# Autocorrelation attention and a merged feed-forward layer: rows added by an accumulating transfer, their low half on GpSimd, statistics' roots in batches, six late folds on TensorE

## The reference, cut

```python
def autocorrelation(Q, K, V):                     # heads H = 8, d = D // H
    corr = ifft(fft(q, axis=2) * conj(fft(k, axis=2))).real
    w, idx = top_k(corr.transpose(0, 1, 3, 2), int(2 * log(L)))
    w = softmax(w)
    for i in range(topk):
        out += w[..., i] * take_along_axis(v, minimum(idx[..., i] + pos, L - 1))

def ffn(x, W, bias, A, Bf, coeffs, scales):
    out = einsum('bsd,od->bso', x, W) + bias
    xa = einsum('bsd,erd->ebsr', x, A)
    return out + einsum('ebsr,eor,e->bso', xa, Bf, coeffs * scales)

x = x + autocorrelation(layernorm(x), ctx_4096, ctx_4096)
x = x + ffn(layernorm(x), L0_ffn_W, L0_ffn_bias, L0_ffn_A, L0_ffn_Bf, L0_ffn_coeffs, L0_ffn_scales)
```

## Time and profile before

| | |
|---|---|
| Median of three executions | 2596.8 us (2594.43 to 2602.17) |
| Profiled execution | 2623.54 us, its span 2621.7 us |
| TensorE busy | 2458.5 us, 94% of the span |
| VectorE, GpSimd, ScalarE busy | 1942.5, 2069.6, 1090.8 us |
| Prelude (windows 0 to 13) | 506.20 us |
| Steady part (windows 14 to 63) | 1823.30 us |
| Tail | 292.20 us |
| TensorE's mean granted clock | 0.98 |

### The profile page before, as it was taken

How to read it: one execution, slowest core, us unless ns; L and a number is a source line. 1 busy time by engine, 2 the same in 40 slices (tenths; PEclk the granted TensorE clock), 3 DMA queues, 4 the chain that set the end, 5 groups by cost and what they waited for, 6 DMA issues and landing times.

```text
span 2621.7 us, 36204 instructions
## 1 busy us (share of the span) xinstructions
PE 2458.5 (94%) x12288; PEld 1534.9 (59%) x12288; DVE 1942.5 (74%) x4526; ACT 1090.8 (42%) x2070; POOL 2069.6 (79%) x1430
## 2 busy tenths in 40 slices
PE   4999866899999979999999999997999999999999
PEld 3666555566666646666666666664666666654444
DVE  5888889778887798778887788779886788645000
ACT  4888856543444333543444344442433344211000
POOL 5799999778998779978997899788797889654222
PEclk8999978899999989999999999998999999999999
DMA  9399998967897677967897689966786687768853
GB/s 328 100 266 270 272 251 199 232 200 223 275 271 211 220 235 236 279 203 225 273 282 209 222 266 284 270 190 203 228 257 183 213 262 246 200 225 288 266 184 113
DMA packets 550025, 613.17 MB, mean 234 GB/s; under 512 B 322640, under 2 KB 448720, under 8 KB 532176
## 3 DMA queue, kind: packets, MB, share of 16 engines
q1 hardware_dynamic: 549840, 610.86, 77.8%
HBM read 383.22 MB, written 151.00 MB: 204 GB/s over the span
## 4 chain that ended last, share of the span: by engine, by line
PE 60%; POOL 16%; DMA 7%; DVE 6%; issue 5%; SPq 4%; ACT 2%; POOLq 0%; DVEq 0%; ACTq 0%
PE f_ps L834 12%; PE f_ps L836 12%; PE f_ps L838 12%; PE a_ps L706 8%; PE a_ps L751 4%; PE a_ps L799 3%; POOL f_x1p L1126 3%; PE a_ps L814 3%; PE a_ps L815 3%; POOL a_zu L1126 2%; POOL a_rows L1126 2%; POOL a_zvf L1126 2%; DMA a_w_lag<-a_w_row 2%; PE a_ps L756 1%; DVE a_twf L1251 1%
## 5 line engine op out<-in xcount | busy, mean ns | idle before, releaser
L834 PE MATMUL f_ps<-f_whi,f_hhi 128*128 128x512 f16 x2048 | 777.1, 379 | 5.8 <-issue 2.3
L836 PE MATMUL f_ps<-f_wlo,f_hhi 128*128 128x512 f16 x2048 | 776.9, 379 | 0.0
L838 PE MATMUL f_ps<-f_whi,f_hlo 128*128 128x512 f16 x2048 | 776.5, 379 | 0.0
L1126 POOL TENSOR_TENSOR a_zvf<-a_zvf,a_twf 128x512 f32<-128x512 f32 x256 | 340.6, 1361 | 115.8 <-DVE a_twf L1251 110.1
L918 ACT ACTIVATE a_side<-a_ps 128x1 f32<-128x1 f32 (+2 forms) x420 | 123.2, 331 | 543.6 <-PE a_ps L795 368.7
L838 PEld LDWEIGHTS f_ps<-f_whi,f_hlo 128*128 128x128 f16 x2048 | 200.6, 98 | 242.2 <-issue 1.1
L836 PEld LDWEIGHTS f_ps<-f_wlo,f_hhi 128*128 128x128 f16 x2048 | 200.6, 98 | 225.3 <-issue 0.8
L834 PEld LDWEIGHTS f_ps<-f_whi,f_hhi 128*128 128x128 f16 x2048 | 200.8, 98 | 219.7 <-issue 5.9
L1126 POOL TENSOR_TENSOR f_x1p<-f_x1p,f_y 128x512 f32<-128x512 f32 x128 | 170.9, 1368 | 100.1 <-DVE f_y L1251 100.1
L918 ACT ACTIVATE a_vu<-a_ps 128x512 f32<-128x512 f32 (+2 forms) x512 | 218.4, 489 | 73.4 <-PE a_ps L706 72.8
L751 PE MATMUL a_ps<-a_w_lag,lags 128*128 128x256 f16 x1536 | 234.8, 277 | 12.7 <-DMA a_w_lag<-a_w_row 11.5
(11 more groups left out here) (134 smaller groups left out, 5054.8 us busy)
## 6 DMA issues: line engine op xcount, KB each, us to landing
f_whi<-whi_scratch SPq DMA_DIRECT2D x128, 512.0 KB, 5.0
f_wlo<-wlo_scratch SPq DMA_DIRECT2D x128, 512.0 KB, 5.9
a_rows<-in_x_dram SPq DMA_DIRECT2D x62, 1024.0 KB, 8.6
vs<-in_ctx_dram SPq DMA_DIRECT2D x64, 512.0 KB, 6.2
xs<-in_x_dram SPq DMA_DIRECT2D x64, 512.0 KB, 7.6
parts_scratch<-a_so SPq DMA_DIRECT2D x64, 512.0 KB, 7.5
x_scratch<-a_rows SPq DMA_DIRECT2D x32, 1024.0 KB, 5.1
f_x1p<-x_scratch SPq DMA_DIRECT2D x32, 1024.0 KB, 6.6
```

Source lines behind the costliest of these rows:

```text
L834: nc.tensor.matmul(f_ps[:, t, :], h_hi[q][:, kq, rows_t], w_hi[u % WR][:, :, kq, :], start=(k == 0), stop=False)
L836: nc.tensor.matmul(f_ps[:, t, :], h_hi[q][:, kq, rows_t], w_lo[u % WR][:, :, kq, :], start=False, stop=False)
L838: mm = nc.tensor.matmul(f_ps[:, t, :], h_lo[q][:, kq, rows_t], w_hi[u % WR][:, :, kq, :], start=False, stop=(k == DB - 1))
L1126: return nc.gpsimd.tensor_tensor(whole, whole, part, op)
```

## The change

Four things change, and a fifth makes room.

1. `add_row` is no instruction of GpSimd any more. One transfer from GpSimd's own queue reads the attention's rows from `parts_scratch` and adds them to `a_rows` (`accum_op=ALU.add`). It is issued between `add_upper` and `add_lower`, and not behind `add_lower`. SP's two `load_attn` transfers per row tile, the tile `f_attn` and their waits go. `row_added` becomes two semaphores that the transfer counts up.
2. `row_low` goes from VectorE to GpSimd, right behind `add_products` and ahead of `add_group`. ScalarE's copy to PSUM goes.
3. `close_statistics` does four tiles at once, with 15 instructions on 128x4, at the end of `weights_low` in windows 5, 13, 21, 29, 37, 45 and 53. Its constants are tiles of SBUF now (`eps4`, `bits4`, `three_halves`), so that every one of these instructions reads two tiles of SBUF.
4. For the values of chunks 8 to 13, GpSimd leaves out the second level of sums and differences (2 instructions), and TensorE multiplies the first level with the matrix twice as often: 8 products and not 4 (`folded_once`, `fold_two`), with two negated matrices more in `fold`.
5. `p_bn`'s tiles lie in `a_side` now.

The core of the diff:

```diff
+UNFOLD_FROM = 8
...
+        def closed_batch(w):
+            if w == 5:
+                return 1
+            return (w - 13) // CHUNKS + 2 if w >= 13 and (w - 13) % CHUNKS == 0 and (w - 13) // CHUNKS < BATCH - 2 else None
...
+        def folded_once(n):
+            return UNFOLD_FROM <= n < LAG
...
             def store_x1(w, r):
-                sp.wait_ge(row_added, r + 1)
+                sp.wait_ge(row_added[w % 2], 16 * (r // 2 + 1))
...
+                if folded_once(n):
+                    fold_two(2, 0, ((0, tv[:, 0, :]), (0, tv[:, 1, :])))
+                    fold_two(2, 1, ((2, tv[:, 2, :]), (4, tv[:, 3, :]))).then_inc(v_mm, 1)
+                    fold_two(3, 0, ((1, tv[:, 2, :]), (1, tv[:, 3, :])))
+                    fold_two(3, 1, ((3, tv[:, 0, :]), (5, tv[:, 1, :]))).then_inc(v_mm, 1)
+                    return
...
-                if r < TB:
-                    act.wait_ge(hi_done, r + 1)
-                    at_least(act, lo_done, r)
-                    copy(f_ps[:, :, :].rearrange("p a c -> p (a c)"), row_hi[:, :]).then_inc(hi_copied, 1)
...
             def add_row(w, r):
                 pool.wait_ge(rows_in[w % 2], 16 * rows_job(w))
-                pool.wait_ge(attn_in, 16 * (r + r // TB + 2))
-                add(rows[w % 2][:, :], attn[:, :], ALU.add).then_inc(row_added, 1)
+                pool.wait_ge(parts_out, 16 * CHUNKS * (r // TB + 1))
+                nc.gpsimd.dma_start(rows[w % 2][:, :], part_rows[r * T:(r + 1) * T, :], accum_op=ALU.add
+                                    ).then_inc(row_added[w % 2], 16)
+
+            def row_low(w, r):
+                pool.wait_ge(hi_done, r + 1)
+                at_least(pool, h_out, 32 * r)
+                nc.gpsimd.tensor_tensor(row_lo[:, :], rows[w % 2][:, :], row_hi[:, :], ALU.subtract).then_inc(lo_done, 1)
...
                     add_products(w)
+                if row_tile(w - 1) is not None:
+                    row_low(w - 1, row_tile(w - 1))
                 if g is not None:
                     add_group(g)
                 if 1 <= w <= N:
                     add_upper(w - 1)
+                if r is not None:
+                    add_row(w, r)
                 if 1 <= w <= N:
                     add_lower(w - 1)
-                if r is not None:
-                    add_row(w, r)
...
+                dve.wait_ge(rows_done, TB * of)
+                dve.wait_ge(q_normed, CHUNKS * (of - 1))
+                link, base = root_link, ROOT_LINKS * (of - 1)
+                nc.vector.scalar_tensor_tensor(out=s_veps[:, :], in0=squares[:, columns], scalar=1.0 / D, in1=eps4[:, :],
+                                               op0=ALU.mult, op1=ALU.add).then_inc(link, 1)
...
             def row_statistics(w, r):
-                dve.wait_ge(row_added, r + 1)
+                dve.wait_ge(row_added[w % 2], 16 * (r // 2 + 1))
...
-                if row_tile(w - 1) is not None:
-                    row_low(w - 1, row_tile(w - 1))
...
                     weights_low(w)
+                close_statistics(w)
```

More of the change, by code:

```diff
@@ L234, in flow @@
         down = sb("p_down", [T, OT])
-        x_bn = [sb(f"p_bn{i}", [T, 4, 6]) for i in range(TB)]
         x_mv = sb("p_mv", [T, TB, 2])
@@ L289, in flow @@
         skew = side
+        x_bn = [side[:, 0, 24 * i:24 * (i + 1)].rearrange("p (a s) -> p a s", s=6) for i in range(TB)]
         top_a = sb("a_top_a", [T, SUB, 8])
@@ L390, in flow @@
         x1_out = sem("f_x1_out")
-        attn_in = sem("f_attn_in")
-        row_added = sem("f_row_added")
+        row_added = [sem(f"f_row_added{i}") for i in range(2)]
         bn_done = sem("f_bn_done")
@@ L639, in _ @@
                 load_x(w + 3)
-                if r is not None and r % TB == 0:
-                    load_attn(r, False)
                 if made:
@@ L706, in fold_matmul, with fold_two @@
                 return nc.tensor.matmul(ps[:, pair, j, :], fold[:, k, :], source, start=True, stop=True)
+            def fold_two(pair, j, terms):
+                for i, (k, source) in enumerate(terms):
+                    mm = nc.tensor.matmul(ps[:, pair, j, :], fold[:, k, :], source, start=(i == 0), stop=(i == 1))
+                return mm
             def values(n):
@@ L1140, in fold_values @@
                 pool.wait_ge(v_lowered, n + 1)
-                nc.gpsimd.tensor_tensor(tv[:, 2:4, :], by_half[:, 0], by_half[:, 1], ALU.subtract
-                                        ).then_inc(v_halved, 1)
-                pool.wait_ge(v_halved, n + 1)
+                halved = nc.gpsimd.tensor_tensor(tv[:, 2:4, :], by_half[:, 0], by_half[:, 1], ALU.subtract)
+                if folded_once(n):
+                    halved.then_inc(v_folded, 1)
+                    return
+                halved.then_inc(v_halved, 1)
+                pool.wait_ge(v_halved, n + 1 - sum(folded_once(i) for i in range(n)))
                 by_half = pairs(tv[:, :, :])
@@ new lines, in close_statistics @@
+                for i in range(3):
+                    at = base + 4 * i
+                    dve.wait_ge(link, at + 2)
+                    nc.vector.tensor_tensor(s_sq[:, :], s_root[:, :], s_veps[:, :], ALU.mult).then_inc(link, 1)
+                    dve.wait_ge(link, at + 3)
+                    nc.vector.tensor_tensor(s_sq[:, :], s_sq[:, :], s_root[:, :], ALU.mult).then_inc(link, 1)
+                    dve.wait_ge(link, at + 4)
+                    nc.vector.scalar_tensor_tensor(out=s_sq[:, :], in0=s_sq[:, :], scalar=-0.5, in1=three_halves[:, :],
+                                                   op0=ALU.mult, op1=ALU.add).then_inc(link, 1)
+                    dve.wait_ge(link, at + 5)
+                    nc.vector.tensor_tensor(gain[:, 0, :] if i == 2 else s_root[:, :], s_root[:, :], s_sq[:, :], ALU.mult
+                                            ).then_inc(link, 1)
```

64 lines of the change are left out of this document (21 added, 43 removed).

## The result

The changed kernel takes 2709.83 us (median of four executions, 2708.32 to 2714.48), 1.0414 times the kernel before (95% interval 1.0361 to 1.0467). The median of the four executions of before that go with it is 2599.49 us, that of 19 later ones 2593.8. The direction was as forecast, the size was not: 19 us were forecast and 110 to 116 came, beyond the range's end of 2650. Its profiled execution took 2714.48 us, with a span of 2712.7 us.

The account below looks back on a forecast made before the run. TensorE was taken to fill whole steady windows of 35.46 us, with waits between ScalarE, VectorE and GpSimd in the prelude. Prelude +5.5, steady part -2.3 and tail +16 gave +19 on 2596.8: 2616 us, range 2570 to 2650.

Parts of the forecast that it names:

- Roots in a batch: Five steady windows with a batch: its instructions wait for GpSimd's, TensorE waits 5.4 us in each; +27 us (0 to 35).
- Window 5: Prelude: the batch stands ahead of a weight tile's scales that ScalarE waits for; +11 us (3 to 14.5).
- window 13: Prelude: its batch of roots put at half of a steady one; +2.5 us (0 to 5).
- the neighbour of 0.21 us: VectorE: a similar instruction's time, taken for each batch instruction without GpSimd; 3.2 us for the fifteen.
- The two long windows: Steady part: windows of 53.30 and 52.96 us fall to 35.46 once VectorE loses the low halves; -35.3 us.
- The even row windows: Twelve steady windows with the accumulating transfer and GpSimd's low half: 0.5 us each, +6 us (0 to +20).
- the sentence on the low half: Even row windows: the subtraction ahead costs GpSimd 4.1 us, some 2 come back, against 2.1 us of cover at TensorE's output.
- The rival of the slow accumulation: Even row windows: transfer lands after 16 us, VectorE's statistics hold the output add; +43 us, 2659 us; chance 0.11.
- The sign named for being wrong: VectorE: the forecast is wrong if statistics wait for the accumulated rows; no size given.
- The tail: Last row tiles: low half ahead of a group's adds delays its store 14 us and SP's queue behind; +16 us (8 to 22).
- the rival of a high half that comes sooner: Tail: GpSimd gets the row's high half 8 us sooner, +16 becomes +8, 2608 us; inside the forecast, no chance of its own.
- The prelude's gain: Prelude: late folds take work from GpSimd, VectorE and ScalarE, about half of 15.2 us comes back; -8 us (0 to -18).

Follow-up runs that it names:

- e1: The changed kernel with the statistics closed tile by tile again, as before the change, all else as changed; 2667.05 us.
- e11: The changed kernel with GpSimd's order group, upper adds, transfer, low half, lower adds, and statistics tile by tile; 2584.04 us, 0.9946 of before.
- e2: The changed kernel with the row's low half behind add_group on GpSimd and not ahead of it; 2647.09 us.
- e3: The changed kernel with the row's addition as a GpSimd instruction again, from a plain load that SP issues; 2671.46 us.
- e10: The changed kernel with GpSimd's order group, upper adds, transfer, low half, lower adds, batched roots kept; 2619.28 us.
- e8: The kernel before with the accumulating transfer alone, without the late folds; 2586.98 us, 0.9973 of before.
- e5: The changed kernel with the low half on VectorE and statistics tile by tile, both as before; 2582.90 us, 0.9946 of before.

## Why the prediction was right and wrong

**Roots in a batch: right.** Instructions end with GpSimd's, a few get through that way, the next waits for the bias add, and TensorE waits behind the output add. 27 us were put on the five windows, 35.0 came: TensorE's own wait was 3.91 us and not 5.4, but the window grew by 7.0, the other 3.1 us being its work at the lower granted clock (1.6 were estimated for that). That was the upper end named (35). Window 5 was put at 11 and is at 13.2 against e1 (33.1); window 13 at 2.5 and is at 5.9 (43.0 against 37.1 in e1). The small chains tile by tile were priced for the steady part alone, at nothing. In the prelude they cost a little: windows 2, 3 and 4 take 32.4 us each without them and 33.0 to 34.1 with them (e1), so in all the two batches cost the prelude 11.0 us. One reading was off without much weight: the neighbour of 0.21 us has one tile and a scalar per partition as inputs, and the batch's own instructions take 0.16. The Trainium skill's rule (SBUF — State Buffer, Who interferes with whom) is that a VectorE instruction with two SBUF inputs contends with a GpSimd instruction that reads SBUF. These rows agree with it: 1.12, 1.19 and 4.43 us for instructions that take 0.16 alone.

**The two long windows: wrong.** The -35.3 us were read from one execution and carried over to the median. Two more profiled executions have no such window, so at the median there was next to nothing to win. (The 17 executions of before that went with e11 reach from 2586 to 2625 us, the 12 of e11 from 2580 to 2586; some of the longer ones may hold such a window, but they have no trace that shows it.) The hint was at hand: the profiled execution lay 26.7 us above the median, and the text explained it by one missing wait of 17.8; two missing waits put the execution at 2588, as near to the 2594 to 2602 of the other three as one does (2606). This step alone turns the sum of +19 into +54.

**The even row windows: wrong, the largest error.** +6 were put there, 52 came (72.3 over against 20.1). Two steps failed together. The first is the sentence on the low half: it counted 4.1 us of GpSimd's time ahead of the lower adds and looked at whether TensorE's output would wait, and did not follow `add_group`, which the same 4.1 us delay, to SP's queue, where the group's store has two 1 MB loads behind it. The same chain was followed in the tail, and not here, though the order of GpSimd and of SP is the same. The second is the transfer: it was taken at 8 to 10 us because the bytes and the engines are the same, its landing was put at nothing because it is issued earlier, and what it does to the transfers beside it is in no term. For the row's store and the statistics that held (16.7 against 16.2 us into the window; waits of 8.4 against 8.2), but it now runs beside these two loads, and they take 3 to 4 us longer. e2, which takes the delay of the group away, gives back 45 us; e3, which takes the transfer away, gives back 24 of 33 in the six windows where no other transfer comes in its place. Of what e2 leaves, e10 takes another 18.4 by issuing the transfer ahead of the low half, and ends below the kernel before (8.7 against 20.1).

**The rival of the slow accumulation** gave 2659 by a transfer of 16 us and an output add that waits behind VectorE's statistics. The transfer lands after 11.0 us in the median, little above the 8 to 10 taken, and in the even row windows TensorE does not wait for the output add. The windows it named are the ones that grew, by another way: the transfer's load on the transfers beside it. The sign named for being wrong, statistics that wait for the accumulated rows, is seen in the tail (87.0 us against 19.2) and not in the steady part.

**The tail: right in kind, too small.** +16 against +30.8. The chain from the group's store to the last row is as described; the row tile's high half was taken from before, at 2413.6, and came 13 us later against window 63 (2487.8 for 2474.9); the rival of a high half that comes sooner is out. What was missed is that the row's transfer is behind the low half of the row before it, so that each row waits for the last one's normalising. e2 takes back 17.3 us, e10 another 10.5.

**The prelude's gain: right.** -8 was put; e1, with no batches, has a prelude of 499.3 us against 506.8 and 508.1 in the two executions of before. The late folds alone are 3.7 of this (e8 to e5); the rest is left for the four low halves and ScalarE's copies, which the term counted too.

By these terms, -7.5 + 11.0 in the prelude, 35.0 + 52.2 in the steady part and 30.8 in the tail, the sum is +121.5, against 120.6 from span to span; the odd row windows, 1.0 us over before and nothing now, make up the difference.

## What to carry to other kernels

When an instruction is moved ahead of another on its engine, follow what the delayed one releases through every queue, in each stage: here 4 us at GpSimd cost 45 us by a store with two loads behind it in SP's order, and in half of the windows only together with another transfer that had moved beside these loads. So when two parts of a change touch the same queue or the same stretch, price them together and not one by one. A gain read from rare long instances (2 of 28) belongs to the execution until a second profiled one shows it too. Small chained instructions with two SBUF inputs go where no one waits behind them; or they stay apart, tile by tile and in the form of before (e1).

## What the runs showed of the hardware

GpSimd's issue of the accumulating transfer takes 0.84 us, and the next instruction starts 0.61 us after the issue did. GpSimd's timeline in window 18 of the changed kernel:

```profile
657.71 0.84 POOL L1198 DMA_DIRECT2D a_rows<-parts_scratch  x1
658.32 5.20 POOL L1127 TENSOR_TENSOR a_zvf<-a_zvf,a_twf 128x512 f32<-128x512 f32 x4
663.23 2.74 POOL L1127 TENSOR_TENSOR a_zu<-a_zu,a_zvf 128x512 f32<-128x512 f32 x2
665.68 1.50 POOL L1159 TENSOR_TENSOR a_tq<-xs 128x512 f32<-128x512 f32 x1
666.91 1.50 POOL L1160 TENSOR_TENSOR a_tq<-xs 128x512 f32<-128x512 f32 x1
668.48 1.27 POOL L1164 TENSOR_TENSOR xs<-a_tq 128x512 f32<-128x512 f32 x1
```

The eight instructions behind the issue are recorded longer: the four adds with 5.20 us (4.93 before), the two behind them with 2.74 (2.50), the folds with 1.50 each. But they start as close to one another as before: 4.91 us from the four to the two, 2.45 from these to the first fold, 1.23 to the second. So a longer record is not lost time here. Nor does it end with the landing: in e10 the transfer issued in window 18 lands 12.6 us into it, and the folds that start at 13.5 and 14.8 are still recorded with 1.49 and 1.48 us.

What the transfer does cost is other transfers' time. In the even row windows SP's load of `f_x1p` takes 6.5 to 7.1 us to landing (medians of the two kinds of windows) in the second execution of before and in e3, and 10.4 to 10.9 in the changed kernel and e10. In e2, where this load is issued 1.4 us ahead of the transfer, it takes 6.5 and 6.6, and the load of `a_rows` behind it 14.9.

The last thing is how differently the same contention falls out. In one execution of the kernel before, a VectorE instruction with two SBUF inputs waited through 18 us of GpSimd's instructions, twice; in two others the same ones took 3.4 us; and a chain of small ones slips in at nearly every end of a GpSimd instruction. What decides which of these happens stays open.
